# A second stage whose norms run in four 64x64 tiles, with all engines' orders rewritten

## What is computed

```python
q = l2norm(q) * qs            # t / max(norm(t over the 64 of a head), 1e-12)
k = l2norm(k) * ksc
q = q * cos * scale + rotate_half(q) * sin * scale
k = k * cos * inv + rotate_half(k) * sin * inv
out = local_attention(q, k, v)        # softmax over a window and the one before it
...
for i in range(DEPTH):                # 6
    x = attn_layer(shift_tokens(x), Wqkv[i], q_scale[i], k_scale[i], Wo[i]) + x
    x = ffn_layer(shift_tokens(x), ln_g[i], ln_b[i], W1[i], b1[i], W2[i], b2[i]) + x
```

## Time and profile before

| | |
|---|---|
| median of 3 runs | 4799.18 us (4795.73 to 4809.79) |
| the profiled execution | 4804.87 us |
| its span | 4803.1 us |
| busy: TensorE, VectorE, GpSimd, ScalarE | 85%, 83%, 73%, 62% of the span |
| first output product of the second stage starts at | 1588.42 us |
| 48th and last starts at | 4759.52 us |

### The profile page before, as it was taken

One profiled execution on the slowest core, in us unless ns is written; L12 is line 12 of the kernel. 1 busy time (PEld: TensorE's weight loads), 2 busy tenths in 40 slices (PEclk: granted clock), 3 DMA queues, 4 the chain that ended last, 5 costly groups with the idle time before them and its releaser, 6 DMA issues.

```text
span 4803.1 us, 153853 instructions
## 1 busy us (share of the span) xinstructions
PE 4079.8 (85%) x60260; PEld 2120.9 (44%) x60260; DVE 3988.7 (83%) x7132; ACT 2994.3 (62%) x4240; POOL 3483.6 (73%) x1655
## 2 busy tenths in 40 slices
PE   3666666666656999999999999999999999999997
PEld 1222332233223455555555555555555555555554
DVE  6999999999974788888888888888888888888885
ACT  5999999999983455545555555555555455554552
POOL 4999899999984676667666676666666676666663
PEclk9755555555557999999999999999999999999998
DMA  0000000000003444444444444454444444454443
GB/s 14 3 6 5 10 5 9 5 10 5 3 7 90 103 103 112 118 119 103 105 117 119 114 103 112 118 126 102 103 117 120 114 101 111 118 127 101 104 115 102
DMA packets 230497, 381.82 MB, mean 79 GB/s; under 512 B 38112, under 2 KB 59232, under 8 KB 229728
## 3 DMA queue, kind: packets, MB, share of 16 engines
q1 hardware_dynamic: 229856, 372.57, 32.1%
HBM read 51.57 MB, written 18.61 MB: 15 GB/s over the span
## 4 chain that ended last, share of the span: by engine, by line
PE 46%; issue 6%; DVE 5%; SPq 4%; POOL 3%; DMA 3%; ACT 2%; DVEq 0%; POOLq 0%
PE pb L1452 11%; PE pb L1510 7%; PE pb L1470 6%; PE pb L1493 6%; PE pb L1457 5%; PE pb L1504 4%; PE pb L1521 3%; SPq L1284 3%; PE pb L1533 3%; POOL sqs L1878 3%; DMA qkn<-early 3%; ACT early L1730 2%; PE pb L1480 2%; DVE early L2015 2%; DVE early L1992 1%
## 5 line engine op out<-in xcount | busy, mean ns | idle before, releaser
L783 POOL TENSOR_TENSOR early<-early 128x1280 f32<-128x1280 f32 x416 | 954.9, 2319 | 141.1 <-ACT early L634 139.4
L1878 POOL TENSOR_TENSOR sqs<-early 128x1024 f32<-128x1024 f32 x192 | 468.6, 2441 | 756.5 <-ACT early L1730 756.5
L634 ACT ACTIVATE early<-S,lam 128x512 f32<-128x512 f32 (+3 forms) x2048 | 951.9, 553 | 84.6 <-DVE lam L927 73.2
L1882 POOL TENSOR_TENSOR early<-early 128x1024 f32<-128x1024 f32 x384 | 947.8, 2486 | 19.0 <-DVE early L1992 17.5
L898 DVE BATCH_NORM_STATS2 stats<-early 128x6 f32<-128x512 f32 (+3 forms) x2048 | 832.3, 478 | 57.4 <-POOL early L783 56.2
L1452 PE MATMUL pb<-early 128*128 128x512 f32 x1536 | 734.9, 606 | 2.6 <-POOL early L1955 2.5
L1991 DVE TENSOR_TENSOR early<-pb,early 128x1024 f32<-128x1024 f32 x384 | 467.4, 1217 | 128.1 <-ACT early L1730 115.1
L1730 ACT ACTIVATE early<-pb 128x1024 f32<-128x1024 f32 x384 | 394.0, 1026 | 269.5 <-PE pb L1452 268.9
L2015 DVE SCALAR_TENSOR_TENSOR early<-rn,early 128x1024 f32<-128x1024 f32 x384 | 513.2, 1357 | 54.6 <-POOL early L1882 50.4
L1735 ACT ACTIVATE lnn<-pb,cst 128x1024 f32<-128x1024 f32 x192 | 212.5, 1107 | 492.7 <-PE pb L1457 492.5
L1893 POOL TENSOR_TENSOR pr<-pr,rsum 128x1024 f32<-128x1024 f32 x192 | 365.2, 1902 | 178.7 <-DVE rsum L2028 178.7
(11 more groups left out here) (122 smaller groups left out, 7371.9 us busy)
## 6 DMA issues: line engine op xcount, KB each, us to landing
qkn<-early SPq DMA_DIRECT2D x1536, 128.0 KB, 2.4
vr<-v SPq DMA_DIRECT2D x96, 768.0 KB, 5.8
vr<-v SPq DMA_DIRECT2D x96, 192.0 KB, 5.5
xr<-hist SPq DMA_DIRECT2D x48, 256.0 KB, 4.8
hist<-xo SPq DMA_DIRECT2D x47, 256.0 KB, 4.7
early<-wqkv SPq DMA_DIRECT2D x24, 384.0 KB, 3.5
early<-hist SPq DMA_DIRECT2D x48, 128.0 KB
vr<-v SPq DMA_DIRECT2D x96, 64.0 KB, 6.3
```

The source lines that it names most:

```text
L634: ins = nc.scalar.activation(W[:, p, h, c], S[:, j % 2, h, c], ACT.Abs_reciprocal_sqrt, bias=lam[:, j, i:i + 1])
L783: nc.gpsimd.tensor_tensor(W[:, p, h, :], W[:, p, h, :], W[:, p, h, :], ALU.mult).then_inc(s_wp[p], 1)
L1878: nc.gpsimd.tensor_tensor(sqs[:, :, :], sq[:, :, 0, :], sq[:, :, 1, :], ALU.add).then_inc(s_sqs, 1)
L1882: nc.gpsimd.tensor_tensor(m1[:, which, :, :], m1[:, which, :, :], m2[:, which, ::-1, :], ALU.add)\
```

## The change

In `norms`, each product of 128x128 is replaced by two products of 64x64 tiles, four tiles for q and k together. For q, the tile at rows 0 to 63 writes to partitions 0 to 63, and the one at rows 64 to 127 to partitions 64 to 127. For k the two are crossed: rows 0 to 63 of the keys' sums land in partitions 64 to 127, and the other way round. In each half of the partitions, one row tile writes to bank 0 and the other to bank 1. The exponential in `inverse_norms` becomes three instructions: one for q, and two of 64 partitions each that write the keys' halves back to their own partitions.

```diff
             def norms(n, g, out):
                 for which in range(2):
-                    mm = pe.matmul(out[:, which, :], ones4[:, :], sqs[:, which, :], start=True, stop=True)
+                    for half in range(2):
+                        i, o = 64 * half, 64 * (half ^ which)
+                        mm = pe.matmul(out[o:o + 64, which, :], ones4[i:i + 64, i:i + 64], sqs[i:i + 64, which, :],
+                                       start=True, stop=True, tile_position=(i, o))
                 mm.then_inc(s_norm, 1)
...
                 act.wait_ge(s_lnn, at(n, g))
-                nc.scalar.activation(rn[:, :, :], lnn[:, :, :], ACT.Exp, scale=-0.5, bias=cst[:, 2:3]).then_inc(s_rn, 1)
+                nc.scalar.activation(rn[:, 0, :], lnn[:, 0, :], ACT.Exp, scale=-0.5, bias=cst[:, 2:3])
+                nc.scalar.activation(rn[0:64, 1, :], lnn[64:P, 1, :], ACT.Exp, scale=-0.5, bias=cst[64:P, 2:3])
+                nc.scalar.activation(rn[64:P, 1, :], lnn[0:64, 1, :], ACT.Exp, scale=-0.5, bias=cst[0:64, 2:3])\
+                  .then_inc(s_rn, 1)
```

More of the change, by code:

```diff
@@ L1349, in body @@
                 if live(b, 0):
-                    rolled(b, 0)
-                if live(b, 0):
-                    load_xr(b)
-                if live(b, 2) and not is_body(b, END + 2):
-                    store(b - 2)
-                if live(b, 1):
-                    load_w1(b - 1, l, k == 1)
+                    rotated(b, 2)
             for b in range(BATCH):
@@ L1636, in body @@
                     scores(b - 1, 3, 0, bank("score3"))
-                if live(b, 0):
-                    take("v1", b)
-                    values(b, 1, bank("v1"))
+                if live(b, 1):
+                    scores(b - 1, 3, 1, bank("score3"))
                 if live(b, 0):
@@ L1862, in _ @@
             act.wait_ge(cleared, 2)
-            for b in range(3):
+            for b in range(4):
                 body(b)
-            with act.Fori(3, STEPS) as b:
+            with act.Fori(4, STEPS) as b:
                 body(b)
@@ L2181, in _ @@
             tables(0)
-            for b in range(3):
+            for b in range(4):
                 body(b)
-            with dve.Fori(3, BATCH) as b:
+            with dve.Fori(4, BATCH) as b:
                 body(b)
```

194 lines of the change are left out of this document (100 added, 94 removed), and 12 rows, old and new, of the table HOLD.

## The result

| | changed kernel | kernel before | ratio, 95% interval |
|---|---|---|---|
| median | 5120.25 us (5097.78 to 5135.74) | 4804.49 us (4795.73 to 4811.02) | 1.0655 [1.0607, 1.0703] |
| profiled execution | 5111.85 us, span 5109.9 | 4804.87 us, span 4803.1 | |

The forecast was 4639 us, and 316 us were lost where 160 were to be won.

The account below looks back on a forecast made before the run. TensorE, 96.6% busy in the second stage, was taken to set the pace. Norms -171, new wait +43, tile shapes -10 and scores' wait -22 gave -160 us, so a median of 4639 us, range 4592 to 4720.

Parts of the forecast that it names:

- A shorter product therefore counts in full, unless an operand then comes too late.: Second stage: TensorE, busy 96.6%, sets the step, so time cut from its products shortens the run in full.
- VectorE's 56.3 us of a step as a fixed amount: Second stage: VectorE's busy time per step, taken from the old kernel; 88% of the forecast 64.1 us step.
- The instructions themselves at nothing: TensorE's norms: priced by columns and microseconds; the sum had no term for the added instructions.
- at the full granted clock: Second stage: TensorE's clock read as full in 38 whole steps of the old kernel; no term for a change.
- The norms at 0.93 us: Norms of each group: four tiles at once take 0.93 us instead of 1.82, -171 us over 192 groups.
- the two last rivals: Norms' tiles: row tiles take turns at a bank, 4810 us (6 in 100); all four in turn, 5156 (3 in 100).
- The exponential at nothing: ScalarE's inverse norms: three instructions cost 1.9 us, 0.75 more per group, covered by idle time and earlier norms.
- The new wait at the norms of group 0, 0.9 us: TensorE waits for GpSimd's sums before group 0's norms, some 0.9 us, 48 times, +43 us.
- The scores' wait for their DMA, gone: Scores of group 3: the 0.46 us wait for their DMA disappears in the new order, -22 us.
- The changes of tile shape, -10 us: Norms beside `weigh`, now in the same tiles: 0.2 us less per step, -10 us, bounds 0 and -20.
- The rival of the chain behind the scores, 4719 us: VectorE's delays reach TensorE and take back half the gain: step 65.8 us, 4719 us, 15 in 100.

## Why the prediction was wrong, point by point

- **"A shorter product therefore counts in full, unless an operand then comes too late."** This is the step that failed. The norms did give their 3.5 us a step, and the rest of the step didn't stay as long as it was. The sum holds +43 us of new wait and -22 us of old, +0.4 in a step. Measured were 8.1 us more of waits in a step, and 2.2 lost to the clock. The waits have the two causes of the next two points.
- **VectorE's 56.3 us of a step as a fixed amount.** This is the larger part. The sum took each VectorE instruction at its duration of before. With `inverse_denominators` directly ahead of `finish`, one instruction became 50% longer, and VectorE needs 61.0 us in a step. Moving three calls behind it returned 206 us. The numbers were there to be read, though not in the rows shown. In the prediction's own step two single `finish` took 1.22 us each, and a pair beside GpSimd more than twice that:

```profile
3038.84 2.76 DVE L2015 SCALAR_TENSOR_TENSOR early<-rn,early 128x1024 f32<-128x1024 f32 x2
```

- **The instructions themselves at nothing.** TensorE can also stop because its next instruction isn't there. The prediction counted columns and microseconds of the norms, not the 32 instructions that four tiles add to a turn. Cutting the norms by columns showed 179 us for these instructions alone. The tiles in one group, with no border shifted, showed the sign that the sum had.
- **"at the full granted clock"** was read from the kernel before and kept for the changed one. There the clock is 0.97 on average, since waits of over 1 us come in every step. By the sum that is 2.2 us of a step, some 104 us in 48. The prediction had no term for it.
- **The norms at 0.93 us:** 0.88 to 1.02. Right, and with it the low chances of the two last rivals. Row tiles that write to one bank in different partitions don't take turns here. The rule cited from the Trainium skill, "TensorEngine Tiling (Array Packing)", section Restrictions and Gotchas, would have made them 1.82.
- **The exponential at nothing:** right in the new order, where the time without the split is the same. The three take 0.72 us each, 2.16 together against a forecast of 1.9. In the old order one wait of 1.3 us stands right behind them, and what it costs there was not run.
- **The new wait at the norms of group 0, 0.9 us:** 0.87 in the step shown, 30.7/39 = 0.8 on average. Right.
- **The scores' wait for their DMA, gone:** right. In the list of waits of the changed kernel none for `qkn` is left. In four steps of the 39 they now wait up to 2.9 us for another DMA, of `hist`.
- **The changes of tile shape, -10 us:** no run measured them apart.
- **The rival of the chain behind the scores, 4719 us:** it named the right engine and the wrong size. It took the waits as what a delayed VectorE hands on, not VectorE itself getting slower. At one group it may have been true: the tiles of group 2 gave 19 us where 0.8 us of norms in 48 steps are 38. Where the other half went was not pursued.
- **Order and place together:** the losses of the tiles with the split exponential (240) and of the order (309) don't add up in the changed kernel (316). With VectorE late, part of the time in which TensorE would wait for instructions is time in which it waits anyway. This is argued from the sums; no run separates it.

Open is the rule by which a piece's fetch starts. In the traces it starts at other instructions than the borders by count would have it, so no formula for a good slot came out of them.

## What to carry to other kernels

When a change adds instructions to an engine that is fed without a gap, count them as well as their microseconds. Look in the trace for idle time that ends with "issue" in the middle of a run of like instructions, and try the kernel before with nothing but a shifted loop, to see what the place is worth. Read the granted clock beside the waits: here it fell behind waits of over 1 us, and with tiles in groups 1 and 2 it cost 2.1 us in a step, more than the new issue wait itself, 1.5. Before an order is rewritten, list the pairs of VectorE and GpSimd instructions that both read their operands from SBUF, and keep them apart: a duration from the profile holds only for the neighbours it had. And try a change first where it shifts nothing: the tiles in one group were faster than before, those in two or four groups slower.

## What the runs showed of the hardware that was not expected

- Moving TensorE's loop by 32 instructions, with nothing else changed, made it 378 us slower (4799.87 to 5177.52). Between two slots of one and the same kernel there were 326 us.
- TensorE's clock fell to half behind waits of over 1 us in the middle of a stage in which it was otherwise full: 66 times in 2700 us with the loop moved, twice before. Two records of 512 columns then take 1.71 us where they take 0.89.
- TensorE uses 256 instructions of the scores in about 1.6 us (an estimate from half a group in 0.79), and 2.0 to 2.9 us pass from the start of a 16 KB fetch to the end of the gap. The gaps are up to 5.6 us long.
- A VectorE instruction with two SBUF operands of 1024 elements takes 1.22 us alone and up to 2.9 beside GpSimd. GpSimd's `normalise` goes from 1.90 to 2.88. With one operand in PSUM, VectorE's stays at 1.22.
- Four 64x64 tiles of 512 columns ran at once, in 0.88 to 1.02 us, though two row tiles wrote to one PSUM bank at the same time, in different partitions.
